# Turning query and keys on VectorE from the fifth sequence on, and storing the attention output in runs of 1 KB

## What is computed

```python
bias = braak_embed[braak_stages][..., None]          # one value per token
q = query + bias                                     # query is x
attn = softmax(einsum('bsd,btd->bst', q, key))       # key is fside
t = einsum('bst,btd->bsd', attn, value)              # value is fside too
nx = t * rsqrt(mean(t * t) + EPS) * norm_w
probs = softmax(nx @ gate_w.T)                       # 8 experts, the best 2 are kept
h1 = base1 + SCALING * low-rank part of each expert  # likewise h3
out = sum over experts of weight * (silu(h1) * h3 @ w2.T + low-rank part)
x = x + out
```

## Time and profile before

| | us |
|---|---|
| median of 3 runs | 1287.82 (1287.31 to 1287.85) |
| the profiled execution | 1289.31 |
| its span | 1287.5 |
| PE busy | 1280.9 (99%) |
| DVE busy | 857.6 (67%) |
| ACT busy | 532.0 (41%) |
| POOL busy | 261.9 (20%) |

### The profile page before, as it was taken

The page is one execution under the profiler, slowest core; times in us unless marked ns, Lnnn a source line. Parts: engine busy times, 40 slices in busy tenths (PEclk is TensorE's granted clock), DMA queues, the critical chain, the costliest instruction groups (busy, mean ns, idle before and its releaser), DMA issues.

```text
span 1287.5 us, 18409 instructions
## 1 busy us (share of the span) xinstructions
PE 1280.9 (99%) x7078; PEld 1117.3 (87%) x7078; DVE 857.6 (67%) x1584; ACT 532.0 (41%) x991; POOL 261.9 (20%) x213
## 2 busy tenths in 40 slices
PE   9999999999999999999999999999999999999998
PEld 8999988888888888888888888888888888888887
DVE  6999766656675576557665667567665766565656
ACT  6888734333333334333433333333433343233332
POOL 2788710202020202002020202020110202020200
PEclk9999999999999999999999999999999999999999
DMA  9899720201102020202020010202020201002000
...
DMA packets 121248, 76.55 MB, mean 59 GB/s; under 512 B 63162, under 2 KB 112200, under 8 KB 121032
## 3 DMA queue, kind: packets, MB, share of 16 engines
...
## 4 chain that ended last, share of the span: by engine, by line
PE 98%; SPq 1%; DVE 1%; DMA 0%; ACT 0%; issue 0%; DVEq 0%
PE bank L1354 31%; PE bank L1355 31%; PE bank L1356 31%; PE bank L1478 2%; PE bank L1462 1%; PE bank L1400 1%; DMA k_pair<-in_fside_BxSxS 0%; PE bank L1366 0%; PE bank L1407 0%; SPq L475 0%; SPq L467 0%; ACT prob L783 0%; SPq L457 0%; PE bank L1449 0%; DVE neg_max L1024 0%
## 5 line engine op out<-in xcount | busy, mean ns | idle before, releaser
L1226 DVE TENSOR_TENSOR act_a<-silu_a,bank 128x512 f32<-128x512 f32 x128 | 87.8, 686 | 211.5 <-PE bank L1356 195.0
L874 ACT ACTIVATE br_hi<-act_br 128x512 fp32r<-128x512 f32 x128 | 81.0, 632 | 187.7 <-DVE act_br L1237 187.7
L867 ACT ACTIVATE silu_b<-bank 128x512 f32<-128x512 f32 x128 | 76.3, 596 | 187.9 <-PE bank L1356 187.1
L691 POOL TENSOR_TENSOR t_lo<-t_in,t_hi 128x512 fp32r<-128x512 f32 x32 | 40.6, 1290 | 552.4 <-ACT t_hi L854 552.2
L1355 PE MATMUL bank<-w2T_lo,s_hi 128*128 128x256 f32 x512 | 144.7, 283 | 0.0
L1356 PE MATMUL bank<-w2T_hi,s_lo 128*128 128x256 f32 x512 | 143.3, 280 | 0.0
L1354 PE MATMUL bank<-w2T_hi,s_hi 128*128 128x256 f32 x512 | 142.7, 279 | 0.0
L1234 DVE TENSOR_TENSOR act_b<-silu_b,bank 128x512 f32<-128x512 f32 x128 | 88.0, 687 | 81.0 <-PE bank L1356 80.0
L863 ACT ACTIVATE silu_a<-bank 128x512 f32<-128x512 f32 x128 | 75.8, 592 | 134.7 <-PE bank L1356 134.6
L710 POOL TENSOR_TENSOR v_lo<-v_full,v_hi 128x512 fp32r<-128x512 f32 x64 | 94.5, 1508 | 136.6 <-ACT v_hi L859 136.6
L1247 DVE TENSOR_TENSOR br_lo<-act_br,br_hi 128x512 fp32r<-128x512 f32 x128 | 104.8, 819 | 5.3 <-ACT br_hi L874 2.8
...
## 6 DMA issues: line engine op xcount, KB each, us to landing
...
x_pair<-in_x SPq DMA_DIRECT2D x52, 128.0 KB, 3.5
k_pair<-in_fside_BxSxS SPq DMA_DIRECT2D x52, 128.0 KB, 3.6
...
```

The lines of the kernel that those rows point to most:

```text
L867: nc.scalar.activation(silu_b[:, :], h1_bank[j % 2][:, :], ACT.Silu).then_inc(silu_b_ready, 1)
L874: nc.scalar.activation(br_hi[j % 2][:, :], act_br[j % 2][:, :], ACT.Copy).then_inc(br_hi_ready, 1)
L1226: nc.vector.tensor_tensor(act_a[j % 2][:, :], silu_a[j % 2][:, :], h3_bank[j % 2][:, :], ALU.mult).then_inc(act_a_ready, 1)
```

## The change

`TURNED` begins with sequence 4. SP's opening loads sequences 4 and 5 as a pair of x and a pair of keys, and the x pair and `bias_rep` come ahead of w2, b1 and b3. kv of 4 and 5 is still loaded, for the values. In `oT` the 256 tokens of a half of the features stand together, with the gate's 8 columns once ahead of them and once behind. The first 128 tokens use the columns ahead, the others those behind, so that each gate product still reads 136 neighbouring columns, and a store has runs of 256 floats. POOL's `add_block_bias` also waits for the q_ready of the sequence before.

```diff
@@ -49,7 +49,7 @@
 GCOLS = GROUP * SC
 BLK = 32
 BLOCKS = S // BLK
-TURNED = range(6, BATCH)
+TURNED = range(4, BATCH)
 RSQRT_SEED = float(0x5F3759DF)
 
 
@@ -124,8 +124,9 @@
         rt = [sb(ctx, f"rt{k}", [P, KT]) for k in range(2)]
 
         sb(ctx, "pad_t", [P, 48])
-        O_STRIDE = P + 32
-        GATE = slice(P, P + E)
+        O_STRIDE = E + S + E
+        LEAD = 32 - E
+        TOKENS = slice(LEAD + E, LEAD + E + S)
         early = ExitStack()
         w1_in = sb(early, "w1_in", [P, FC, D])
         w3_in = sb(early, "w3_in", [P, FC, D])
@@ -149,7 +150,7 @@
         value = [split(f"value{k}", [P, SC, D], early) for k in range(2)]
         probT = [split(f"probT{k}", [P, SC * S], early, ((16, 16), (32, 48))[k]) for k in range(2)]
         sb(early, "pad_probT", [P, 16])
-        oT = [sb(early, f"oT{k}", [P, DC, SC, O_STRIDE]) for k in range(2)]
+        oT = [sb(early, f"oT{k}", [P, DC, O_STRIDE + 2 * LEAD]) for k in range(2)]
         gram_diag = sb(early, "gram_diag", [P, SC, P])
         bias_rep = sb(early, "bias_rep", [P, BLOCKS, BATCH])
         opening = ExitStack()
@@ -359,7 +360,8 @@
         def job_bank(n):
             return gate_bank if n == EXTRA_JOB else w_bank[n % 2]
 
-        GATE_STRIDE = P + E
+        def gates_of(ap):
+            return ap.rearrange("p (n e) -> p n e", e=E)[:, ::O_STRIDE // E - 1, :]
 
 
         DVE_BIAS = 4
@@ -477,8 +479,7 @@
 
             def store(c):
                 sp.wait_ge(oT_copied, c + 1)
-                sp.dma_start(t_scratch[bass.ds(P * c, P), :].rearrange("p (n s) -> p n s", s=P).rearrange(
-                             "p (d h) s -> p d h s", d=DC), oT[c % 2][:, :, :, 0:P]
+                sp.dma_start(t_scratch[bass.ds(P * c, P), :].rearrange("p (d s) -> p d s", d=DC), oT[c % 2][:, :, TOKENS]
                              ).then_inc(t_stored[c % 2], 16)
 
             def store_rows(r):
@@ -489,9 +490,9 @@
                 sp.dma_start(scale_scratch[:, cols], scale_rows[:, :]).then_inc(rows_stored, 16)
 
             def step(c):
-                if c % 2 == 0 and c + 4 in TURNED:
+                if c % 2 == 0 and c + 4 < BATCH:
                     load_x_pair(c + 4)
-                if c % 2 == 1 and c + 3 in TURNED:
+                if c % 2 == 1 and 6 <= c + 3 < BATCH:
                     load_k_pair(c + 3)
                 if 6 <= c + 3 < BATCH:
                     load_kv(c + 3)
@@ -511,18 +512,18 @@
             sp.dma_start(w3_in[:, :, :], w3.rearrange("(p j) d -> p j d", j=FC)).then_inc(w3_loaded, 16)
             load_xs(3)
             load_kv(3)
-            load_xs(4)
             sp.wait_ge(bias_copied, 1)
             sp.dma_start(bias_scratch.rearrange("(h p) b -> p h b", p=P), bias[:, :, :]).then_inc(bias_stored, 16)
-            sp.dma_start(w2_in[:, :, :], w2.rearrange("(c p) f -> p c f", p=P)).then_inc(w2_loaded, 16)
-            sp.dma_start(b1_in[:, :, :], b1.rearrange("e (p j) r -> p e (j r)", j=FC)).then_inc(b_loaded, 16)
-            load_kv(4)
-            load_xs(5)
-            sp.dma_start(b3_in[:, :, :], b3.rearrange("e (p j) r -> p e (j r)", j=FC)).then_inc(b_loaded, 16)
+            load_x_pair(4)
             sp.wait_ge(bias_stored, 16)
             for g in range(P // BLK):
                 sp.dma_start(bias_rep[g * BLK:(g + 1) * BLK], bias_scratch.rearrange("(j s) b -> s j b", s=BLK)
                              ).then_inc(bias_rep_loaded, 16)
+            load_k_pair(4)
+            sp.dma_start(w2_in[:, :, :], w2.rearrange("(c p) f -> p c f", p=P)).then_inc(w2_loaded, 16)
+            sp.dma_start(b1_in[:, :, :], b1.rearrange("e (p j) r -> p e (j r)", j=FC)).then_inc(b_loaded, 16)
+            load_kv(4)
+            sp.dma_start(b3_in[:, :, :], b3.rearrange("e (p j) r -> p e (j r)", j=FC)).then_inc(b_loaded, 16)
             load_kv(5)
             for c in range(1, SCALED_STEPS[0]):
                 step(c)
@@ -645,6 +646,7 @@
                                         ).then_inc(value_lo_ready, 1)
 
             def add_block_bias(c):
+                pool.wait_ge(q_ready, c)
                 pool.wait_ge(bias_rep_loaded, 16 * P // BLK)
                 pool.wait_ge(x_pair_loaded[pair_at(c)], pair_count(c))
                 blocks = as_blocks(x_in[c % RING][:, :, :]).rearrange("p (j n) -> p j n", j=BLOCKS)
@@ -672,7 +674,7 @@
             def place_gate(k):
                 pool.wait_ge(gate_w_copied, 1)
                 for dc in range(DC):
-                    last = nc.gpsimd.tensor_copy(oT[k][:, dc, :, GATE],
+                    last = nc.gpsimd.tensor_copy(gates_of(oT[k][:, dc, LEAD:LEAD + O_STRIDE]),
                                                  gateT[:, dc, :].unsqueeze(1).to_broadcast([P, SC, E]))
                 last.then_inc(gate_placed, 1)
 
@@ -793,8 +795,8 @@
                 act.wait_ge(o_ready, c + 1)
                 if c >= 2:
                     act.wait_ge(t_stored[c % 2], 16 * (c // 2))
-                nc.scalar.activation(oT[c % 2][:, :, :, 0:P].rearrange("p d h s -> p (d h) s"),
-                                     o_bank[:, :].rearrange("p (n s) -> p n s", s=P), ACT.Copy).then_inc(oT_copied, 1)
+                nc.scalar.activation(oT[c % 2][:, :, TOKENS], o_bank[:, :].rearrange("p (d s) -> p d s", d=DC),
+                                     ACT.Copy).then_inc(oT_copied, 1)
 
 
             def exp_gap(r):
@@ -1033,11 +1035,10 @@
 
                 dve.wait_ge(gate_ready, c + 1)
                 cols = bass.ds(SC * c, SC)
-                halves = gate_bank[:, 0:SC * GATE_STRIDE].rearrange("p (h n) -> p h n", h=SC)
                 for h in range(SC):
-                    nc.vector.scalar_tensor_tensor(gram_diag[:, h, :], halves[:, h, 0:P], 1.0 / D, ident[:, :],
-                                                   ALU.mult, ALU.mult, accum_out=mean_sq[:, SC * c + h:SC * c + h + 1])
-                nc.vector.tensor_scalar(logits[:, cols, :], halves[:, :, GATE], 1.0, None, ALU.mult
+                    nc.vector.scalar_tensor_tensor(gram_diag[:, h, :], gate_bank[:, E + h * P:E + (h + 1) * P], 1.0 / D,
+                                                   ident[:, :], ALU.mult, ALU.mult, accum_out=mean_sq[:, SC * c + h:SC * c + h + 1])
+                nc.vector.tensor_scalar(logits[:, cols, :], gates_of(gate_bank[:, 0:O_STRIDE]), 1.0, None, ALU.mult
                                         ).then_inc(gate_read, 1)
 
 
@@ -1475,8 +1476,9 @@
 
             def gate_half(c, h):
                 for dc in range(DC):
-                    last = nc.tensor.matmul(gate_bank[:, h * GATE_STRIDE:(h + 1) * GATE_STRIDE],
-                                            oT[c % 2][:, dc, h, 0:P], oT[c % 2][:, dc, h, 0:GATE.stop],
+                    last = nc.tensor.matmul(gate_bank[:, h * (E + P):(h + 1) * (E + P)],
+                                            oT[c % 2][:, dc, LEAD + E + h * P:LEAD + E + (h + 1) * P],
+                                            oT[c % 2][:, dc, LEAD + h * (E + P):LEAD + (h + 1) * (E + P)],
                                             start=(dc == 0), stop=(dc == DC - 1))
                 if h == SC - 1:
                     last.then_inc(gate_ready, 1)
```

## The result

The kernel after the change takes 1290.88 us (median of 12 runs, 1289.30 to 1293.58), the kernel before, run beside it, 1287.32 (12 runs, 1286.45 to 1289.05): a ratio of 1.0029, interval 1.0021 to 1.0037. The forecast was 1287.0 with a range up to 1289.4, so the time lies outside it, above 1290.4, to which the text had given 0.05. The profiled execution of the kernel after took 1290.01 us, 0.9 under the median; it ran from the span's 1288.2 us plus 1.8, the same surplus as before.

What follows compares the result with a forecast made beforehand. PE was taken to bound the attention phase, with transfers close behind. Terms of -1.9 (turns), +2.3 (SP's queue) and -1.2 (stores) summed to -0.8 us, giving a median of 1287.0, range 1284.9 to 1289.4.

Steps and rivals of the forecast that it cites:

- what the change removes on PE: Steps 3 and 4: without PE's transposes of q and kv both become like step 5, 1.9 us less.
- what it does to SP's queue: Opening loads, steps 3 to 5: later transfers make DVE wait 3.2 us for k_pair 6, costing 2.3 us.
- the hole: DMA queue in the opening: idle time behind SP's wait for bias_stored, put at 1.0 us, between 0 and 2.5.
- POOL: POOL's added block bias and turned q_low: hidden if x_pair 6 lands in time, at 33.1, barely covered; costed at nothing.
- the shift worked out for k_pair 6: SP's queue: loads land 3.3 - 0.2 + 1.0 us later, less 0.7 idle filled; k_pair 6 goes from 35.5 to 38.9.
- The sign of being wrong that the prediction had named: POOL waiting for x_pair 6 or b_in so that scores(5) wait for qT_lo, costed at nothing.
- The sum priced a wait at its length less 0.9 us: From step 27, where 2.13 us of DVE's waiting lengthened the step by 1.24: 0.9 us of a wait is covered.
- the stores: Stores up to step 27: longer runs save 1.4 us of DMA time, cutting the k_pair wait; 1.2 us less, ends 0 and 1.24.
- the loss in step 27: Step 27 took 5.45 us against 4.21 in step 26, with DVE waiting 2.13 us for k_pair; all 1.24 comes back.
- The third rival: Slower: bias_stored wait starves SP's queue, k_pair 6 after 41, DVE waits 5.4, stores give nothing; +2.6, 1290.4; chance 0.08.

Runs made afterwards that it cites:

- e16: As e12, but POOL's copy of b1 waits for b1 alone and its copy of b3 comes a step later: 1289.83 us, ratio 1.0015.
- e6: The change with the bias's store issued behind the rest of w1 instead of behind kv 3: 1290.47 us, ratio 1.0023 against the kernel before.
- e7: The change with store 0 issued ahead of b3 and kv 5: 1291.23 us, ratio 1.0027 against the kernel before.
- e9: The change with store 0 replaced by an equal-sized transfer from w1's tile ahead of x_pair 4, so ACT need not wait: 1290.71 us, ratio 1.0028.
- e14: The kernel of e7 run again for another profile: a single run of 1290.57 us.
- e4: The change run again, unaltered, for a second profile: 1291.95 us, ratio 1.0036 against the kernel before.
- e5: The kernel before, unchanged, run for a second profile: one run of 1288.16 us.
- e2: The change without its stores (turning and SP's new opening, old oT layout, 512 B runs): 1290.78 us, ratio 1.0027 against the kernel before.
- e1: The kernel before with only the new oT layout and 1 KB store runs, turning from sequence 6 on: 1286.21 us, ratio 0.9995.
- e15: The change run again, unaltered, for a further profile: a single run of 1291.11 us.
- e17: The kernel of e1 run again for a narrower interval: 1287.51 us, ratio 0.9999 against the kernel before.
- e13: The change run again, unaltered, to profile an execution with a lower mean clock: a single run of 1291.94 us.
- e3: The change with w2 issued between x_pair 4 and SP's wait for bias_stored: 1289.88 us, ratio 1.0018 against the kernel before.
- e12: The change with earlier bias store and bias_rep, transfers in due order, b1/b3 copies a step later, a2 behind k_pair 8, b2 later: 1291.47 us, ratio 1.0024.

## Why the prediction was wrong

**Step "what the change removes on PE", -1.9: right.** Step 3 is 5.07 or 5.08 in every profile of the change, and e16, where all loads of this stretch are in time, has all four steps at 5.07 to 5.11.

**The step that failed: "what it does to SP's queue", where it says who waits.** It named the first stores among what is queued behind the wait, and gave them no waiter and no price; k_pair 6 was the only load that cost anything, +2.3 in step 5, and step 4 was to be 5.1 us. But ACT's copy of oT 2 has to wait until store 0 has read its buffer. Store 0 landed at 32.8 to 34.5 where it had landed at 26.8, ACT waited 2.67 to 5.91 us, and step 4 took 6.88 to 10.76 us: 1.8 to 5.7 us that the sum did not have. Every instruction that is queued behind a wait has to be followed to its own waiter, the stores too.

**The rest of that step: the place right, the cause of the hole wrong, the price high.** The hole was put at 1.0 us and blamed on the wait for bias_stored. It is 2.2 us, and e6 leaves 1.8 of it without that wait; SP stood 6.3 us at x_pair 4's issue. k_pair 6 was put at 38.9 and landed at 40.3 to 42.0. DVE's wait was put at 3.2 and was 1.7 to 2.3, only because step 4 had been stretched already. Step 5 lost 1.8, 2.1, 1.2 and 0.9 us.

**Step "POOL": the landing wrong, the price right for another reason.** x_pair 6 was put at 33.1 by the shift worked out for k_pair 6, and called barely covered. It landed at 35.1, and POOL waited 2.68: the estimate took issues in a queue as running on at their old pace, and SP had stood 3.32 us at kv 5, just ahead. The sign of being wrong that the prediction had named, scores(5) waiting for qT_lo, is in none of the change's four profiles, since ACT's longer wait covered it. It appears in e7, e9 and e14 (2.36 to 2.41 us), where that wait is shorter or gone. That the forecast of nothing held in the change is luck.

**Missing: what a long wait does to the clock.** The sum priced a wait at its length less 0.9 us. That held in step 4 of the first profile and of e4. After PE had stood for 2.63 and 3.88 us, 0.5 and 0.6 us more went.

**Step "the stores", -1.2: not shown.** It took the loss in step 27 of one execution (1.24 us) for that of all, and put it down to the stores' runs. In other profiles the loss is 0.54 (e5) and none (e2) with the old stores, and with the new ones none (e1, e4, e15, e17), 0.4 (the change's first), 0.6 (e13) and 1.0 (e3, e12). The wait is there with either, and what sets it is open. Part of the loss was also counted twice: what the profiled execution lost there beyond a typical one (0.7 us more than e5) is in the 1.5 us by which it exceeded the median, and that 1.5 was taken off as well. The medians of e1 and e17 cannot decide between nothing and a small gain. The Trainium skill (DMA: Bandwidth & Descriptors, Specifications) puts the least transfer for line rate at 512 B. By that rule the term would be zero, and no run here shows it to be anything else.

The sum with sizes as measured, for steps 3 to 6 of the four profiles against the 22.2 before: -1.8 for the turns (22.2 less e16's 20.4), and +3.5, +4.6, +5.6 and +6.6 for steps 4 and 5. That is +1.7, +2.8, +3.8 and +4.8, 3.3 on average, and the medians say +3.6. The third rival ended nearest: a landing of k_pair 6 from 41 on came true in three of the four profiles, the stores gave nothing that shows, and its 1290.4 is 0.5 under the measured time. Its mechanism was another, one DVE wait of 5.4 us, where there were two shorter waits in a row and the larger was ACT's.

No version beat the kernel before beyond the interval: e1 and e17 are level with it, e16's best runs are not under its best. Why most runs of e16 are 2 us or more over its one profile stays open.
